# Every second adjacency product of the first rank stage as three one-pass products

## What is computed

```
R = adj + I;  R = R / rowsum(R)
for n in range(2):
    probs = softmax((Xa W1' W2') (Xa W3')')      # 4096 x 4096
    A = probs where it belongs to the smallest set of largest entries
        with mass 0.9 (top-p), else 0;  A = A / rowsum(A)
    Xf = R Xf;  Xa = A Xa
    Z += Xf U1[n]' + Xa U2[n]'
out = layernorm(x + (layernorm(x + Z) * g + b))
```

## Time and profile before

| | |
|---|---|
| time, median of 3 runs | 1669.39 us (1666.16 to 1671.97) |
| the profiled execution | 1669.76 us, span 1668.0 us |
| PE / DVE / ACT / POOL busy | 92% / 76% / 47% / 15% of the span |
| HBM traffic | 127 GB/s over the span |
| mean granted TensorE clock | 0.956 |

### The profile page before, as it was taken

How to read it: one execution, slowest core, us unless ns; L and a number is a source line. 1 busy time by engine, 2 the same in 40 slices (tenths; PEclk the granted TensorE clock), 3 DMA queues, 4 the chain that set the end, 5 groups by cost and what they waited for, 6 DMA issues and landing times. The chain is left out here.

```text
span 1668.0 us, 17981 instructions
## 1 busy us (share of the span) xinstructions
PE 1527.7 (92%) x4753; PEld 883.6 (53%) x4753; DVE 1267.6 (76%) x3735; ACT 780.0 (47%) x1237; POOL 247.9 (15%) x283
## 2 busy tenths in 40 slices
PE   7999999978999999998999999998168888899996
PEld 4565555534555555554565656565134444555553
DVE  5788878723677777776899999998968787787664
ACT  4555555412555656554444444444034434444444
POOL 2010210241000000001001111122310222322322
PEclk9999999989999999998999999999579999999998
DMA  7466656654355555555556766771000000000000
GB/s 252 170 173 152 157 156 187 195 190 160 145 195 179 192 208 208 190 184 206 192 141 197 202 177 179 192 182 57 2 2 1 1 8 7 1 7 7 7 7 13
DMA packets 53452, 211.94 MB, mean 127 GB/s; under 512 B 22464, under 2 KB 31232, under 8 KB 32880
## 3 DMA queue, kind: packets, MB, share of 16 engines
q1 hardware_dynamic: 49872, 210.61, 40.6%
q0 software_dynamic: 3488, 0.31, 0.2%
HBM read 206.64 MB, written 4.50 MB: 127 GB/s over the span
## 5 line engine op out<-in xcount | busy, mean ns | idle before, releaser
L1289 ACT ACTIVATE psL<-psL,umax 128x1024 f32<-128x1024 f32 x256 | 278.5, 1088 | 301.4 <-DVE umax L1812 301.1
L1818 DVE MAX8 cand<-psL 128x8 f32<-128x256 f32 (+1 forms) x640 | 371.4, 582 | 61.0 <-PE psL L916 54.6
L915 PE MATMUL psL<-kA,mq 128*128 128x512 f32 x512 | 300.1, 586 | 3.0 <-ACT psL L1289 1.6
L885 PE MATMUL psO<-adj_in,xn 128*128 128x512 f32 x512 | 243.2, 597 | 4.4 <-DMA adj_in<-in_adjT 2.2
L885 PE MATMUL psO<-adj_in,xf 128*128 128x512 f32 x512 | 242.1, 597 | 4.4 <-POOL adj_in L611 4.4
L1097 PE MATMUL psO<-ebuf,xn 128*128 128x512 f32 x512 | 241.5, 593 | 0.5 <-DVE ebuf L2029 0.5
L2029 DVE SCALAR_TENSOR_TENSOR ebuf<-ebuf 128x1024 f32<-128x1024 f32 x128 | 156.7, 1225 | 108.2 <-PE psO L1097 92.0
L1449 ACT ACTIVATE ebuf<-psL 128x1024 f32<-128x1024 f32 x128 | 130.4, 1022 | 186.9 <-PE psL L1143 157.9
L916 PE MATMUL psL<-kB,mq 66*128 66x512 f32 x512 | 204.6, 400 | 0.0
L1398 ACT ACTIVATE ebuf<-psL 128x1024 f32<-128x1024 f32 x128 | 131.0, 1024 | 129.1 <-PE psL L1064 128.7
L1155 PE MATMUL psO<-xf,xa 128*128 128x512 f32 x340 | 164.4, 606 | 6.4 <-DVE xf L2182 6.2
(11 more groups left out here) (341 smaller groups left out, 1961.5 us busy)
## 6 DMA issues: line engine op xcount, KB each, us to landing
adj_in<-in_adjT SPq DMA_DIRECT2D x128, 1024.0 KB, 5.2
adj_in<-in_adj SPq DMA_DIRECT2D x32, 2048.0 KB, 7.6
xaT<-in_xT SPq DMA_DIRECT2D x4, 512.0 KB, 5.2
xa_dram<-xa SPq DMA_DIRECT2D x8, 256.0 KB, 7.7
out<-t SPq DMA_DIRECT2D x8, 256.0 KB, 2.3
list_dram<-ids,place POOLq DMA_INDIRECT x64, 9.5
rel_prob<-cut_dram SPq DMA_DIRECT2D x32, 2.0 KB
cut_dram<-ncut SPq DMA_DIRECT2D x16, 2.0 KB, 8.7
```

Source lines behind the costliest of these rows:

```text
L885: last = nc.tensor.matmul(psO[:], fs[:, j, :], adj_in[:, r % RING, j % JQ, :], start=(j == 0), stop=(j == JT - 1))
L915: nc.tensor.matmul(o, qA[:, t * P:(t + 1) * P], kA[:, c:c + BI], start=True, stop=False)
L1289: nc.scalar.activation(ps[:], ps[:], ACT.Exp, bias=umax[:, bass.ds(i * UB + k, 1)], scale=1.0, accum_out=usum[:, bass.ds(i * UB + k, 1)]). ...
L1818: last = v.max(cand[:, t % 2, at + c * 8:at + c * 8 + 8], psL[(turn + k) % 3][:, c * WIDE:(c + 1) * WIDE])
```

## The change

In the first six blocks of the adjacency product of the first step, each even j (of the first block only those from 8 on) is split, 92 parts in all. ScalarE copies the part to fp32r (`split_hi`, which rounds it) into one of nine buffers, GpSimd subtracts the rounded part from the part and writes the rest in fp32r over the part (`split_lo`; `part_lo` lies on `adj_in`), and TensorE multiplies rounded x with the rounded part, the rest of x with the rounded part, and rounded x with the rest. x itself is split in four pieces in units 3 to 6 (`piece_hi`, `piece_lo`), into buffers that lie where `ebuf` and `xa` are used later. ScalarE's copy of a part stands in its program behind the exponential of the unit four before the one in which the part is used (LEAD = 4), and waits there for the load. GpSimd's list stores are spread over four units, and the subtractions stand among them. Some semaphores are merged (`w_ps` with `w_sb`, `h_flag` with `h_flags` in the first step).

```diff
+        HI_RING = 9
+        def part_hi(n):
+            return (halves[:, 0, :], halves[:, 1, :], halves[:, 2, :], part_his[:, 8, :], part_his[:, 9, :],
+                    part_his[:, 10, :], part_his[:, 5, :], part_his[:, 6, :], part_his[:, 7, :])[n % HI_RING]
...
+        LEAD = 4
+        PIECES = (1, 2, 3, 0)
+        PIECE_AT = {FLOW_FROM + n: n for n in range(NU)}
+        def is_split(a, j):
+            return a < FLOWS and j % 2 == 0 and (a > 0 or j >= JT // NU)
...
+        SELF_AT = {USED_AT[a, a * JQ] - LEAD - 2: a for a in range(FLOWS)}
+        def splits_at(unit):
+            return [n for n, part in enumerate(SPLITS) if max(USED_AT[part] - LEAD, FLOW_FROM + NU) == unit]
...
+                def split_lo(n):
+                    a, j = SPLITS[n]
+                    part = adj_in[:, j // JQ % RING, j % JQ, :]
+                    pool.wait_ge(g["split_hi"], NU + n + 1)
+                    pool.sem_inc(met, 1)
+                    nc.gpsimd.tensor_tensor(part_lo[:, j // JQ % RING, j % JQ, :], part, part_hi(n).bitcast(FP32),
+                                            ALU.subtract).then_inc(g["split_lo"], 1)
...
-                    for i in range(NB):
-                        for a in SELF_BEFORE.get(i, ()):
-                            add_self(a)
-                        list_rows(i)
+                    add_self(0)
+                    for unit in range(NB * UB):
+                        if unit in PIECE_AT:
+                            piece_lo(PIECE_AT[unit])
+                        if unit in SELF_AT and SELF_AT[unit] > 0:
+                            add_self(SELF_AT[unit])
+                        since = unit - UB + 1
+                        if since >= UB and since % UB < TB:
+                            list_part(since // UB - 1, since % UB)
+                        for m in splits_at(unit):
+                            split_lo(m)
+                    for t in range(1, TB):
+                        list_part(NB - 2, t)
+                    list_rows(NB - 1)
...
-                    last = nc.tensor.matmul(psO[:], fs[:, j, :], adj_in[:, r % RING, j % JQ, :],
-                                            start=(j == 0), stop=(j == JT - 1))
+                    if s == 0 and is_split(i, j):
+                        n = SPLIT_NO[i, j]
+                        c = slice(j * P, (j + 1) * P)
+                        pe.wait_ge(g["split_hi"], NU + n + 1)
+                        nc.tensor.matmul(psO[:], x_hi[:, c], part_hi(n), start=(j == 0), stop=False)
+                        pe.wait_ge(g["split_lo"], NU + n + 1)
+                        nc.tensor.matmul(psO[:], x_lo[:, c], part_hi(n), start=False, stop=False)
+                        last = nc.tensor.matmul(psO[:], x_hi[:, c], part_lo[:, r % RING, j % JQ, :],
+                                                start=False, stop=(j == JT - 1))
...
+                def split_hi(n):
+                    a, j = SPLITS[n]
+                    act.wait_ge(g["adj_in"][j // JQ % RING], adj_loads(s, a, j // JQ))
+                    if j // JQ == a:
+                        act.wait_ge(g["self_in"], (a + 1) * TB)
+                    if n >= HI_RING:
+                        b, m = SPLITS[n - HI_RING]
+                        act.wait_ge(g["adj_used"], b * PARTS + m // JQ + 1)
+                    nc.scalar.copy(part_hi(n), adj_in[:, j // JQ % RING, j % JQ, :]).then_inc(g["split_hi"], 1)
...
+                            if s == 0:
+                                if i * UB + k in PIECE_AT:
+                                    piece_hi(PIECE_AT[i * UB + k])
+                                for n in splits_at(i * UB + k):
+                                    split_hi(n)
```

More of the change, by code:

```diff
@@ L112, in gnn_kernel, with first @@
         norm_dram = [nc.dram_tensor(f"norm_dram{s}", [P * T, 1], FP32, kind="Internal").ap() for s in range(STEPS)]
+        with ExitStack() as rounded:
+            def first(name, shape):
+                return rounded.enter_context(nc.sbuf_tensor(name, shape, FP32R))
+            x_hi = first("x_hi", [P, N])
+            x_lo = first("x_lo", [P, N])
+            part_lo = first("part_lo", [P, RING, JQ, BI])
+            part_his = first("part_his", [P, NB + 3, BI])
+        ebuf = sb("ebuf", [P, 4, UNIT])
+        xa = sb("xa", [P, T, D])
+        adj_in = sb("adj_in", [P, RING, JQ, BI])
+        xf = sb("xf", [P, T, D])
+        oT = sb("oT", [D, BI])
+        yn = sb("yn", [P, TB, D])
+        t2 = sb("t2", [P, TB, D])
         xn = sb("xn", [P, T, D])
-        xa = sb("xa", [P, T, D])
-        xf = sb("xf", [P, T, D])
         z = sb("z", [P, T, D])
@@ L377, in gnn_kernel @@
         assert len(ROWS_AT) == FLOWS - 1 and len(set(unit // UB for unit in ROWS_AT)) == FLOWS - 1
+        LEAD = 4
[3 more added lines that the diff above has]
+            return a < FLOWS and j % 2 == 0 and (a > 0 or j >= JT // NU)
+        USED_AT = {}
+        for unit in range(NB * UB):
+            for j in flow_parts(unit)[1]:
+                USED_AT[flow_parts(unit)[0], j] = unit
+        SPLITS = [(a, j) for a in range(FLOWS) for j in range(JT) if is_split(a, j)]
+        SPLIT_NO = {part: n for n, part in enumerate(SPLITS)}
+        SELF_AT = {USED_AT[a, a * JQ] - LEAD - 2: a for a in range(FLOWS)}
+        def splits_at(unit):
+            return [n for n, part in enumerate(SPLITS) if max(USED_AT[part] - LEAD, FLOW_FROM + NU) == unit]
         def k_bank(u):
@@ L650, in tile_fetch, with list_part @@
                             bounds_check=N - 1, oob_is_err=False).then_inc(g["h_ref"], 16)
-                def list_rows(i):
[L654 to L660, removed]
+                def list_part(i, e):
+                    t = i * TB + e
+                    pool.wait_ge(g["st_place"], i + 1)
+                    nc.gpsimd.indirect_dma_start(
+                        out=list_dram[s], out_offset=bass.IndirectOffsetOnAxis(ap=place[:, t:t + 1], axis=0),
+                        in_=ids[:, t, :], in_offset=None,
+                        bounds_check=N - 1, oob_is_err=False).then_inc(g["listed"], 16)
@@ new lines, in list_rows, with piece_lo @@
+                def list_rows(i):
+                    for e in range(TB):
+                        list_part(i, e)
+                def piece_lo(n):
+                    pool.wait_ge(g["split_hi"], n + 1)
+                    pool.sem_inc(met, 1)
+                    c = slice(PIECES[n] * UNIT, (PIECES[n] + 1) * UNIT)
+                    nc.gpsimd.tensor_tensor(x_lo[:, c], xn[:].rearrange("p t d -> p (t d)")[:, c], x_hi[:, c].bitcast(FP32),
+                                            ALU.subtract).then_inc(g["split_lo"], 1)
@@ L1044, in _ @@
                     with pe.Fori(0, tiles) as c:
[L1045 to L1046 removed]
+                        pe.wait_ge(g["h_flag"], 2 * c + 1)
+                        nc.tensor.matmul(psS[:, 0:1], ones[:], hflag[:], start=True, stop=True).then_inc(g["h_flag"], 1)
                         pe.wait_ge(g["h_mid"], c + 1)
@@ L1220, in _ @@
         def _(act):
-            act.wait_ge(w_ps, 1)
+            act.wait_ge(w_made, 1)
             nc.scalar.copy(wq[:, 0:DA], psQ[:, 0:DA])
-            nc.scalar.copy(wq[:, DA:P], psQ[:, 0:DA]).then_inc(w_sb, 1)
+            nc.scalar.copy(wq[:, DA:P], psQ[:, 0:DA]).then_inc(w_made, 1)
             for s in range(STEPS):
```

31 lines of the change are left out of this document (17 added, 14 removed).

## The result

The changed kernel takes **1692.91 us** (median of 4 runs, 1689.93 to 1693.82), the kernel before 1669.64 beside it (4 runs, 1666.16 to 1671.97): a ratio of 1.0144, with a 95% interval of 1.0126 to 1.0162. It is slower by 23 us. The prediction said slower as well, but 1677 us, and its range ended at 1688. The profiled execution took 1693.82 us, its span 1692.0; that of before had 1668.0, so the two traces differ by 24.0 us.

A forecast was written before the change was run, and what follows sets the result against it. TensorE was taken to pace the first rank stage, with a loop of cuts and late loads behind it. 8.2 us gained against 15.9 of VectorE delay: 7.7 slower than 1669.8, stated as 1677 us; range 1660 to 1688.

The forecast's parts named there:

- the loop of the late loads: From cut to cut in the first rank stage, through late load and ScalarE's copy: 37.6 us against 37.9 before.
- TensorE's gain, 14.3 us: First rank stage: 92 fp32 products of 0.86 us become three one-pass ones of 0.235, 0.155 less each, 14.3 us.
- ScalarE's copies, 0.58 us and hidden: 92 copies of 128x512 on ScalarE, 0.58 us each, 53 us more, 7 us a block on 20.8: it fits.
- the last three blocks still gain 0.3 us each: Last three loops from cut to cut: TensorE stalls 1.4 us, so a block gains 0.3 us and not 1.9.
- Where the loop binds: Last three loops, late parts wanted in units 80, 96, 112; of the three before, only the last loses about 0.8 us.
- A hold of 0.8 us at every second split, 3 us a block: GpSimd's subtractions lock out VectorE's two-input statistics steps: about 3.5 hits of 0.8 us a block, 3 us.
- The way of the holds: VectorE's holds make the cut 2.5 us later against TensorE, and this goes round the loop of the cut.
- What the holds cost, 15.9 us: VectorE's delay of the cut: seven blocks times 2.5 us, less 1.6 us of room in the first two loops.
- The light lock: Rival: VectorE's holds delay a cut by only 0.5 to 2 us, giving 1669 us; chance 0.25.
- the full gain: Rival: parts land in time or the three banks absorb ScalarE's wait: -14.3, 1655.5 us; chance 0.06.
- The rival with only the loop: Rival: cuts keep their place in unit 12, only the late load costs: -8.2, 1661.5 us; chance 0.17.
- The rival with GpSimd as the bound: Rival: subtractions take 2.3 us, GpSimd 35 us a block, TensorE waits for remainders: about 1687 us; chance 0.10.

The follow-up runs named there:

- experiment 5: Changed kernel without GpSimd's 92 subtractions (rest of each split part missing from the result) and with a cut's stores issued one adjacency load later: 1656.38 us, ratio 0.9929.
- experiment 1: Changed kernel without the 92 subtractions on GpSimd, third product multiplying the rounded half again; copies, load waits and three products stay: 1675.14 us, ratio 1.0035.
- experiment 3: Changed kernel with the stores of a cut issued one adjacency load later, subtractions kept: 1680.85 us, ratio 1.0058.
- experiment 11: Changed kernel with each subtraction made as two of 256 columns, one behind the other, all work kept: 1697.2 us, ratio 1.0161.
- experiment 10: Changed kernel with GpSimd's subtraction replaced by a zero fill of 128x512 that reads nothing from SBUF: 1673.94 us, ratio 1.0023.

## Why the prediction was wrong

The direction was right, and both causes that the prediction named are real, the late load in front of ScalarE's copy and VectorE's steps held by GpSimd's subtractions. The size was not: 23.3 us where 7.7 were forecast, and beyond the range. Three steps failed: the sum of the loop of the late loads (-8.2 forecast, +5.1 measured), the way and the price of the holds (15.9 us by way of the cut; 18.2 to 25.0 measured, the larger with the cut's late load away), and the clock, which had no term.

- **TensorE's gain, 14.3 us: right.** Experiment 5 shows 14.2 by the medians, 8 to 16 by the ratio. The weight loads of a split part in the changed kernel stand as those of the earlier trace rows did for the logits:

```profile
97.22 0.19 PEld L956 LDWEIGHTS psO<-halves,x_hi 128*128 128x128 f32 x1
97.45 0.19 PEld L958 LDWEIGHTS psO<-halves,x_lo 128*128 128x128 f32 x1
97.69 0.19 PEld L959 LDWEIGHTS psO<-part_lo,x_hi 128*128 128x128 f32 x1
```

- **ScalarE's copies, 0.58 us and hidden: right** in what they cost by themselves (0.61 us long, nothing to be seen of them in the time of experiment 5). The waits for the loads came eight times, up to 4.5 us each and 17.2 in all, where six were named.
- **Only the loop of the late loads, -8.2 us: wrong, it is +5.1** (experiment 1). The step that failed is the sum of the loop, and in it the term that the last three blocks still gain 0.3 us each. Against experiment 5 the stretch is 14.1 us longer, where the step allowed 14.3 - 8.2 = 6.1: TensorE stands still for 8.2 us more, since the loads behind a cut took 14.3 and 15.4 us there and not the 13.1 of the earlier trace rows, 5.1 us are the clock, and 0.8 is left. The other 5 us of the 19.3 between the two kernels lie outside the stretch. What comes after unit 127 takes between 1346 and 1355 us in the traces, in kernels that differ in little or nothing there, so no cause can be given for them.
- **Where the loop binds: right.** The first two cut distances of experiment 1 are 36.5 and 36.1 us, the later ones over 38.
- **A hold of 0.8 us at every second split, 3 us a block: right in kind, it is 6 us a block.** In block 2 of the changed kernel the subtraction starts 1.9 to 2.1 us after the end of the maximum (1.83 predicted), and VectorE's steps behind the maxima of units 37, 39 and 42 are held by 0.81, 0.95 and 1.05 us. But there are 48 holds in seven blocks and not 3.5 in each: the three subtractions of that place met a step each, not every second one. And six holds of over 1.4 us make 15.4 of the 42.4 us. The prediction took GpSimd's instructions one at a time, and a hit at 1.14 us at most; in a row, between list stores and identity additions, they cost one step 1.5 to 4.7 us. Without these six it would still be 3.9 us a block.
- **The way of the holds: not the one named, or not that one alone.** The prediction let the hold delay the cut, by 2.5 us a block, and sent that "round the loop of the cut". With that loop loosened the subtractions still cost 25.0 us (experiment 3 against 5). They reach TensorE within a unit or two, by way of the maximum and the exponential, as at 312.78 us.
- **What the holds cost, 15.9 us: too little.** With the late loads there, the subtractions cost 18.2 (23.3 - 5.1). Alone they cost 25.0 (experiment 3 against 5), and the late loads alone 19.3 (experiment 1 against 5). Both together cost 37.5, where the prediction had 15.9 + 6.1 = 22.
- **The clock: not in the prediction at all.** It is 10.2 us of the 37.5, and none in experiment 5.
- **The rivals.** The light lock and the full gain are excluded. The rival with only the loop was run as experiment 1 and was itself 13 us too low. The rival with GpSimd as the bound came nearest by its number, 1687, but by another mechanism. GpSimd didn't become the bound: TensorE waits for remainders 2.2 us in the stage, and a subtraction takes 1.28 us as forecast:

```profile
L717 POOL TENSOR_TENSOR part_lo<-adj_in,part_his 128x512 fp32r<-128x512 f32 x60 | 76.8, 1280 | 97.3 <-ACT part_his L1333 97.0
```

## What to carry to other kernels

Price a stall of TensorE with what comes behind it. In the stretches of all traces together, 29 of the 42 stalls of 1.3 to 3.3 us had a fall of the clock behind them, the longer stalls more often, for 1.7 us more each and sometimes 3.4; filling the stalls with products of zeros took that back. Before giving GpSimd work that reads SBUF, look at which VectorE steps with two inputs will stand beside it, at its worst queue and not at one instruction, and start it where VectorE turns to a read of PSUM. A wait on an engine that had none before, put ahead of its other work, makes latencies matter that were free. Move out of the way first what lengthens them, in this case three small stores ahead of a load.

## What the runs showed of the hardware

- TensorE's granted clock fell to 0.50 behind stalls of 1.4 to 3.3 us, for 3.4 or 6.8 us, and behind others of up to 2.05 us it didn't (experiment 11 has both the shortest with a fall, 1.35 us, and the longest without one). What decides between them these runs don't show.
- A VectorE step with two SBUF inputs is held by a GpSimd subtraction, not by a fill of 128x512 (0.53 us) nor by a list store alone. A one-input copy is held by both subtraction (0.98 us for 0.17) and fill (0.53).
- A held step can stay held over several GpSimd instructions in a row (4.85 us for a step of 0.16), and sometimes a step gets in between. In the 3.19 us hold above it began during the list store that stood ahead of two subtractions, though a list store with no reading instruction behind it held nothing in experiment 10. What decides this is open.
- A 1 MB load issued right behind the three small stores of a cut landed 12.7 to 15.4 us after its issue in the kernels before and after and in experiment 1, a load with nothing ahead of it in 4.8. The load after it, issued 4 to 6 us later, took 10.0 to 10.9 us in four cases of these traces.
